# Selective scan: the 16 state products of a batch taken step by step beside the output products of the batch before and the projections and convolution of the batch after

## The reference, cut to what matters

```python
xz = jnp.einsum('bld,ed->ble', x, in_proj_w)          # x is the normed input
x_inner, z = jnp.split(xz, 2, axis=-1)
xc = conv_general_dilated(transpose(x_inner), conv_w, ...)   # 4 taps, by channel
x_conv = _silu(xc + conv_b)
x_dbl = jnp.einsum('bld,ed->ble', x_conv, x_proj_w)
delta = softplus(x_dbl[..., 0]); B_ssm = x_dbl[..., 1:17]; C_ssm = x_dbl[..., 17:]
A = -jnp.exp(A_log)
def step(h, inp):
    x_t, d_t, B_t, C_t = inp
    h = h * jnp.exp(d_t[:, None, None] * A) + x_t[:, :, None] * (d_t[:, None, None] * B_t[:, None, :])
    return h, jnp.einsum('bdn,bn->bd', h, C_t)
y = scan(step) + x_conv * D
return jnp.einsum('bld,od->blo', y * _silu(z), out_proj_w)   # added to the stream
```

## Time and profile before

| | us |
|---|---|
| time before, median of 3 runs | 3537.13 (3536.32 to 3538.09) |
| the profiled execution's own time | 3562.51 |
| its span in the profile | 3560.8 |
| selective scan stage, first DMA issue to the last add to X | 1750.9 to 2098.6 |
| busy PE, DVE, ACT, POOL over the span | 2774.7, 1910.1, 1357.7, 927.1 |
| mean granted TensorE clock | 0.88 |

### The profile page before, as it was taken

How to read it: one execution, slowest core, us unless ns; L and a number is a source line. 1 busy time by engine, 2 the same in 40 slices (tenths; PEclk the granted TensorE clock), 3 DMA queues, 4 the chain that set the end, 5 groups by cost and what they waited for, 6 DMA issues and landing times. The chain is left out here.

```text
span 3560.8 us, 32341 instructions
## 1 busy us (share of the span) xinstructions
PE 2774.7 (78%) x10146; PEld 1384.6 (39%) x10146; DVE 1910.1 (54%) x3671; ACT 1357.7 (38%) x1980; POOL 927.1 (26%) x608
## 2 busy tenths in 40 slices
PE   2048898999999899999877776682999999388317
PEld 1024444555555544444344452351333333056203
DVE  6556522222222466565544459112677777589687
ACT  1023332111111156666543320241677877343003
POOL 0014663000000000000122210303699999300005
PEclk7568998999999899999878879896999999689558
DMA  2011121000000165554200020112000000100001
GB/s 53 0 31 43 49 59 29 0 0 0 0 0 0 42 138 141 143 142 144 76 1 1 0 74 0 36 53 73 10 1 1 10 1 1 33 1 1 2 0 30
DMA packets 107456, 126.07 MB, mean 35 GB/s; under 512 B 22283, under 2 KB 60300, under 8 KB 107052
## 3 DMA queue, kind: packets, MB, share of 16 engines
q1 hardware_dynamic: 105260, 120.13, 12.8%
q0 software_dynamic: 2048, 4.20, 0.4%
HBM read 108.55 MB, written 14.16 MB: 34 GB/s over the span
## 5 line engine op out<-in xcount | busy, mean ns | idle before, releaser
L2394 PE MATMUL dots_x<-all_xt,delta_wE 128*128 128x512 f32 x768 | 364.0, 610 | 3.6 <-DVE dots_g L2489 2.2
L2379 POOL TENSOR_TENSOR dots_pr<-dots_g 128x512 f32<-128x512 f32 (+2 forms) x96 | 305.5, 3204 | 64.0 <-DVE dots_g L2489 56.2
L1046 DVE SCALAR_TENSOR_TENSOR attn_sim<-attn_sc,attn_mask 128x512 f32<-128x512 f32 (+3 forms) x256 | 125.8, 491 | 317.0 <-PE attn_sc L972 313.8
L972 PE MATMUL attn_sc<-attn_q,attn_xb 128*128 128x512 f32 (+3 forms) x768 | 295.0, 486 | 0.0
L983 PE MATMUL attn_op<-attn_sim,attn_v 128*128 128x512 f32 (+3 forms) x768 | 295.0, 486 | 0.0
L1332 DVE TENSOR_TENSOR grp_h<-grp_sq,grp_cb 128x512 f32<-128x512 f32 x256 | 176.4, 691 | 189.5 <-ACT grp_sq L1220 170.8
L1160 PE MATMUL grp_po<-grp_h,grp_down 128*128 128x512 f32 x512 | 265.1, 600 | 5.8 <-DVE grp_h L1332 5.8
L1152 PE MATMUL grp_ph<-all_xt,grp_up 128*128 128x512 f32 x512 | 263.3, 597 | 0.5 <-ACT grp_sg L1236 0.5
L2486 DVE TENSOR_TENSOR dots_m<-dots_x,dots_sg 128x512 f32<-128x512 f32 x256 | 173.8, 688 | 149.0 <-PE dots_x L2394 142.8
L1214 ACT ACTIVATE grp_r<-grp_ph 128x512 f32<-128x512 f32 x272 | 162.4, 597 | 183.1 <-PE grp_ph L1152 181.4
L2394 PEld LDWEIGHTS dots_x<-all_xt,delta_wE 128*128 128x128 f32 x768 | 135.2, 189 | 233.2 <-issue 138.6
(11 more groups left out here) (623 smaller groups left out, 4868.7 us busy)
## 6 DMA issues: line engine op xcount, KB each, us to landing
grp_cb<-grp_combine SPq DMA_DIRECT2D x512, 128.0 KB, 3.1
mix_cb<-top_weights SPq DMA_DIRECT2D x64, 256.0 KB, 3.2
cap_xs<-cap_zero SPq DMA_DIRECT2D x7, 320.0 KB, 4.8
experts_xe<-cap_xs SPq DMA_DIRECT2D x7, 320.0 KB, 3.3
all_x<-in_L_attn_x_dram SPq DMA_DIRECT2D x4, 512.0 KB, 5.1
cap_w<-in_L_ffn_W_dram SPq DMA_DIRECT2D x1, 2048.0 KB
cap_ys<-experts_yo SPq DMA_DIRECT2D x8, 256.0 KB, 2.3
delta_h<-all_xn SPq DMA_DIRECT2D x1, 2048.0 KB
```

What stands on the lines that cost most here:

```text
L972: nc.tensor.matmul(sc[k % SC][:, 0:w], xb[:, m * P:(m + 1) * P], q[:, par, n0:n0 + w], start=True, stop=True).then_inc(s_mm, 1)
L2379: nc.gpsimd.tensor_tensor(slot[w % SLOTS][:, at:at + n], a_, b_, ALU.mult).then_inc(pool_ready, 1)
L2394: nc.tensor.matmul(bank(n, sh)[:], wE[:, 1 - k % 2, a, sh], XTj[:, k // 2, par::2], start=True, stop=True).then_inc(u_mm, 1)
```

## The change

The functions are cut into single pieces, and the pieces of back(b-1) and of project(b+1) and conv(b+1) are put between the 16 steps of states(b), at steps given by small tables:

- PE: after the sum and the spread of step n come, for n in 0, 2, 4, 6, one x projection of batch b+1; for n in 1, 3, 5, 7, one of the four groups of products of batch b-1 (L1641 and L1643 of before); for n in 11 to 14, a quarter of the output products of b-1 (L1650 of before).
- DVE: after G of step n come, for n in 3, 5, 7, 9, the add of x times D (and, after 5 and 9, the product with z); for n in 6, 8, 10 to 15, one tap of the convolution of b+1. The add to X of batch b-1 comes after mask(b).
- ACT: after E of steps 0, 2, 4 and 6 comes the copy of one x half of b+1. After states(b) come the conv Silu of b+1 and then the four z halves of b+1.
- PE: the four z projections of b+1 stand behind states(b). The first two wait until batch b-1 has been added to X, since they write the banks from which DVE adds.

Batches 1 and 2 carry both kinds of side work, batch 3 only the outputs of batch 2, batch 0 none. Batches 0 and 1 are projected as before; the outputs of batch 3 follow at the end as before.

```diff
+    IN_AT, TURN_AT, OUT_AT = (0, 2, 4, 6), (1, 3, 5, 7), (11, 12, 13, 14)
+    SKIP_AT, CONV_AT = (3, 5, 7, 9), (6, 8, 10, 11, 12, 13, 14, 15)
...
-                def project(b):
-                    for n in range(8):
...
-                        if b >= 2 and n < 2:
-                            pe.wait_ge(x_added, 2 * (b - 1))
+                def project(b, n):
...
+                    if b >= 2 and n in (4, 5):
+                        pe.wait_ge(x_added, 2 * (b - 1))
...
+                def beside(b, n):
+                    if b < 0:
+                        return
+                    if b + 2 < BATCH and n in IN_AT:
+                        project(b + 2, IN_AT.index(n))
+                    if n in TURN_AT:
+                        turned_states(b, *divmod(TURN_AT.index(n), 2))
+                    if n in OUT_AT:
+                        output(b, OUT_AT.index(n))
...
                 def states(b):
...
                         nc.tensor.matmul(acc[:], ident[:], G[:, n % 2], start=(n == 0), stop=(n == N - 1)).then_inc(sum_mm, 1)
                         if n + 2 < N:
                             spread(n + 2)
+                        beside(b - 1, n)
...
                 for b in range(BATCH):
                     states(b)
+                    if 1 <= b < BATCH - 1:
+                        for n in range(4, 8):
+                            project(b + 1, n)
                     if b + 1 < BATCH:
                         front(b + 1)
-                    back(b)
-                    if b + 2 < BATCH:
-                        project(b + 2)
...
                         nc.scalar.activation(E[:, n % 2], dsb[:], ACT.Exp, scale=negA[:, n:n + 1]).then_inc(E_ready, 1)
+                        if 1 <= b < BATCH - 1 and n in IN_AT:
+                            take_x(b + 1, IN_AT.index(n))
...
                 for b in range(BATCH):
                     states(b)
+                    if 1 <= b < BATCH - 1:
+                        take_conv(b + 1)
+                        take_z(b + 1)
                     if b + 1 < BATCH:
                         front(b + 1)
-                    if b + 2 < BATCH:
-                        project(b + 2)
...
                         tt(G[:, n % 2], cb[n % 2][:], EB[:, n % 2], ALU.mult).then_inc(G_ready, 1)
+                        if b:
+                            beside(b - 1, n)
...
                 for b in range(BATCH):
                     states(b)
                     mask(b)
+                    if b:
+                        add_out(b - 1)
                     if b + 1 < BATCH:
                         front(b + 1)
-                    back(b)
-                    if b + 2 < BATCH:
-                        conv(b + 2)
```

More of the change, by code:

```diff
@@ L1627, in states @@
                             spread(n + 2)
[L1629 to L1653, removed]
+                        beside(b - 1, n)
+                for n in range(8):
+                    project(0, n)
                 front(0)
-                project(1)
+                for n in range(8):
+                    project(1, n)
                 for b in range(BATCH):
                     states(b)
+                    if 1 <= b < BATCH - 1:
+                        for n in range(4, 8):
+                            project(b + 1, n)
                     if b + 1 < BATCH:
                         front(b + 1)
-                    back(b)
-                    if b + 2 < BATCH:
-                        project(b + 2)
+                for k in range(CT):
+                    for g in range(2):
+                        turned_states(BATCH - 1, k, g)
+                for pair in range(4):
+                    output(BATCH - 1, pair)
             @block.scalar
@@ L1676, in _, with take_x, take_z, take_conv @@
                 act.wait_ge(padded, 1)
-                def project(b):
-                    for n in range(8):
+                def take_x(b, n):
+                    k, half = divmod(n, 2)
+                    act.wait_ge(pj_mm, b * 8 + n + 1)
+                    if b >= 2:
+                        act.wait_ge(conv_done, CT * (b - 1))
+                    nc.scalar.activation(xin[:, b % 2, k, PAD + half * GROUP:PAD + (half + 1) * GROUP], pj[n % 2][:], ACT.Copy).then_inc(pj_copied, 1)
+                def take_z(b):
+                    for n in range(4, 8):
                         k, half = divmod(n, 2)
                         act.wait_ge(pj_mm, b * 8 + n + 1)
[L1682 to L1689, removed]
+                        if b >= 2:
+                            act.wait_ge(y_ready, CT * (b - 1))
+                        nc.scalar.activation(z[:, b % 2, k - CT, half * GROUP:(half + 1) * GROUP], pj[n % 2][:], ACT.Silu).then_inc(pj_copied, 1)
+                def take_conv(b):
                     for k in range(CT):
@@ L1855, in back, with beside @@
                         tt(X[:, t0:t0 + TPG], pj[half][:].rearrange("p (t c) -> p t c", c=C), X[:, t0:t0 + TPG], ALU.add).then_inc(x_added, 1)
-                conv(0)
+                def beside(b, n):
+                    if n in SKIP_AT:
+                        k, g = divmod(SKIP_AT.index(n), 2)
+                        skip(b, k, g)
+                        if g:
+                            gated(b, k)
+                    if b + 2 < BATCH and n in CONV_AT:
+                        conv(b + 2, CONV_AT.index(n))
+                for step in range(CT * TAPS):
+                    conv(0, step)
                 front(0)
-                conv(1)
+                for step in range(CT * TAPS):
+                    conv(1, step)
                 for b in range(BATCH):
```

89 lines of the change are left out of this document (62 added, 27 removed).

## The result

| | us |
|---|---|
| before, median of 4 runs | 3537.51 (3536.32 to 3538.09) |
| after, median of 4 runs | 3558.00 (3556.81 to 3559.79) |
| ratio, 95% interval | 1.0059 (1.0043 to 1.0075) |
| forecast | 3562.6 (3541 to 3583), slower 0.82 |
| profiled execution after, own time and span | 3557.2, 3555.5 |

The change costs 20.5 us, 0.6%. The profiled execution of before had 3562.5, so the two profiles can't be subtracted as wholes. The scan stage can: from its first DMA issue to its last add to X it took 347.7 us before and 368.8 after, 21.1 more, and that agrees with the medians. The other difference lies behind the scan; the last experiment shows where.

What follows compares the result with a forecast made beforehand. It took PE and POOL as full in steady steps, with waiting around them to win; batch 1 +15.2, batch 2 +13.2, batch 3 -2.9 give +25.5 on the profiled 3562.5, or 3562.6 us on the median, range 3541 to 3583.

Steps and rivals of the forecast that it cites:

- The loops: States of batches 1 and 2, steps 0 to 7: 8.1 us to sum 1, then 8.25 per pair of steps, sum 7 at 32.8.
- the ring: Steps 0 to 7: x copy waits for PE's projection, E queued behind it, then EB, G and PE's next sum wait in turn.
- The clock: PE's waits of about 3.5 us bring back 1.2 GHz: 1.7 us in each of four bursts and the z projections, 8.5 a batch.
- The z tail: Behind the states of batches 1 and 2: z projections wait for the adds to X, 3.5 us, plus 1.7 for the clock.
- DVE against POOL: Steps 8 to 15 of batches 1 and 2: convolution taps and POOL's EB take turns, 2.1 us a batch, bounds 0 and 6.4.
- The 2.37 a step: A tap of 1.31 and an EB of 1.06 in turn, against DVE's 2.03: 0.35 us more in each of six steps.
- the row: Profile row from elsewhere in the kernel: a DVE product took 2.18 beside a POOL product (1.22 alone), and POOL's 1.94 instead of 1.06.
- The table load: ACT's exponential table load moves from ahead of E into front(2) and front(3), behind the x_proj products: +1.3 us each.
- Batch 3: States without x copies, first E to the end of the mask: 33.1 against 38.0 us, less 2.0 for the clock: -2.9.
- The end: Batch 3's mask to the last add to X: expected to keep its order, change 0.
- The sign named for being right: From the end of the hst copy to the next front, 66 to 69 us in batches 1 and 2.
- The other signs: E in pairs 8 to 10 us apart, sums at 2.08, slow taps or EB, z projections waiting, batch 3's states 33 to 36.

Runs made afterwards that it cites:

- the last experiment: The kernel before, unchanged, profiled once more on another chip: span 3560.2 us, median of its runs there 3562.3 us.
- late: The changed kernel with ACT's four x copies behind the exponentials of steps 5, 7, 9, 11 instead of 0, 2, 4, 6: 3520.6 us.
- onelate: The changed kernel with each x copy one exponential later, behind E(1), E(3), E(5), E(7): 3529.9 us.
- warm: The changed kernel with 12 extra bf16 products behind each x projection in steps 0, 2, 4, 6, into a buffer nobody reads then: 3546.5 us.
- after_table: The changed kernel plus a one-column exponential behind the last Silu of z, loading ACT's table early: ratio to before 1.0046, on another chip.
- tuned: The changed kernel with later x copies, z projections in the spread C rows' buffers, early exponential table, and side work rebalanced over the steps: 3514.8 us.
- late_table: The changed kernel with x copies behind E of steps 5, 7, 9, 11 and the early exponential table: ratio to before 0.9936, on another chip.

## Why the prediction was right, and where its sizes were not

**The loops: right.** Predicted pitch 8.25 at full clock and 1.7 a burst; measured 10.0, 10.7, 9.9 and 8.2 for the four, together 38.8 to sum 7. late shows that the ring is the cause, onelate its formula, and warm its two parts: 34.6 without most of the clock loss.

**The clock: right in kind, and in sum partly by luck.** The prediction's four bursts stand at sums 1, 3, 5 and 7. Up to the start of sum 7 that gives 32.8 and three bursts, 37.9, and 38.8 was measured. But 1.9 of the excess of 6.0 lies before sum 1 (10.0 against 8.1), where the prediction had no loss and the lower level was still that of front(1). The loss isn't spread evenly, as the term assumed: from sum 1 to sum 2 it is 2.7 (5.48 against 2.82), from 3 to 4 1.6 (4.45), from 5 to 6 only 0.1 (2.93) and from 7 to 8 1.8 (4.62), with 3.15 to 3.21 us of waiting before each. In batch 2 it is 1.8, 1.8, 1.5 and 0.1, and the granted clock there was 0.50 for 3.3 us in each of the first three bursts and 1.00 from 2009 to 2032.8, through the fourth. The z tail took 5.3 where 5.2 was summed (3.5 + 1.7). The Trainium skill ("TensorE: Matmul & The Clock Gate", "HAM oscillation — how this bites in real kernels") has the lower clock return at every burst of such a loop. Here the granted clock fell to 0.50 in five of the eight bursts, was low throughout one, and stayed at 1.00 in two, by these rows.

**DVE against POOL: this step failed, 2.1 for nothing measured.** From the end of G(7) to that of G(15) the sum was 15.9 without the term and 18.0 with it. Batch 1 took 16.9, but this holds a wait of DVE of 1.7 for the product group of step 7, which ran at the lower clock. Batch 2, where that group ran at the full clock, took 15.5, and both batches of warm 15.4. In all four EB went up to 2.04. The 2.37 a step assumed that each engine waits for the other. In the trace it is EB that is stretched (up to 2037 ns, where it starts 0.2 us behind a tap), and at a pitch of 1.9 to 2.0 it still fits: the lower bound of the term, 0, was the right value. The lock that the Trainium skill states ("SBUF — State Buffer", "Who interferes with whom") is there, by EB at 2037 ns, but the row, in which both were slow, was no price for these taps.

**The table load: right**, 1.1 and 1.2 for 1.3, and shown by after_table.

**Batch 3: right**, -3.5 for -2.9; nine of the ten variants took 34.5 to 35.3 there, tuned with its other tables 36.9.

**The end: missed, +1.6.** The last 32 output products took 5.47 where the same 32 took 3.84 before, after the same idle 2.10. PE's order around them didn't change; the prediction had this piece at nothing. All ten variants have 16.2 from mask to last add, and both profiles of before have 14.6, so it belongs to the new order and not to one execution. It is the clock: from 2111.4 on, 0.7 us into these products, the granted clock was 0.50 for 3.3 us, after 37 us at 1.00, where before it was 1.00 throughout (2062 to 2102). The prediction's clock term, taken at the loops and the z tail, had nothing for this burst. Why the clock falls here after the same waits as before stays open.

**The sum.** +11.9 + 9.0 + 2.3 - 3.5 + 1.6 - 0.2 (everything up to the hst copy of batch 1) = +21.1, against +25.5. Batch 1 is 2.0 under its term: 1.1 lie between G(7) and G(15), 0.8 in the loops, where the 1.7 for sum 7 belongs to the piece behind. Batch 2 is 2.9 under, 2.5 of it between G(7) and G(15), its loops 39.6 as summed. The fronts are 0.3 under, batch 3 0.6, and the end 1.6 over. The sign named for being right, 66 to 69 us from the hst copy to the next front, was missed for this reason: 64.8 and 63.9. The other signs held, with one pitch of 10.7 where 8 to 10 was said. The errors partly cancel: without the 1.6 of the end, which had no term, the sum would lie 6.0 under the forecast and not 4.4.

## What to carry to other kernels

A copy out of PSUM put into an engine's list "beside" a pipeline is only beside it if what is queued behind the copy isn't needed to produce what the copy waits for. Go round the ring and add its links; where it is longer than the work in it, move the copy later in the list until it is shorter: here one place gave 5.36 against 4.75 of work, five places left PE without a gap in steps 4 to 7, and four moved copies took the kernel from 0.6% slower to 0.5% faster. And price the waits of a matmul pipeline twice, once for the wait and once for the clock behind it.

## What the runs showed of the hardware

- Unneeded products paid: 96 bf16 products of 512 columns more, and 11.5 us less, since the sums behind a 3.15 us gap run at 1.02 instead of up to 2.08 when the gap is filled.
- The same gap doesn't always cost: 3.15, 3.15, 3.16 and 3.21 us before the bursts at sums 1, 3, 5 and 7 of batch 1, and these sums take 2.08, 1.13, 1.13 and 1.81 (the group behind sum 3 is slow too, that behind sum 5 not). The first of them was at the lower level since before its gap.
- POOL and DVE on SBUF: EB 1058 to 2037 ns beside taps that go from 1276 to 1356. In the other direction a short DVE product, W, went from 424 to 1491 ns beside a POOL product that started 0.05 us before it, and a tap took 1.96 us in tuned and the product with z 1.60 us in onelate, 0.6 and 0.5 us behind the start of one. In all these rows it was the instruction that started second that took much longer.
- The kernel before had 3537.5, 3538.3 and 3537.9 at the median in three comparisons and 3562.3 on the chip of the last, 22.9 us of it in one wait for a DMA. The scan doesn't differ like that: late, and late_table on that chip, have stretches of 44.3 and 45.3, and of 44.3 and 44.3.
